# Gate broadcasts of a fused audio tower: source row in SBUF in place of a DRAM scratch

## What is computed

```
h = conv(x)                                   # 8 x 735 x 64
h = h + attention(layernorm(h))
z = layernorm(h)
logits = z @ gate_w + gate_b                  # 16 experts, the best 2 taken
topk_w = softmax(top 2 logits)
hidden = relu(z @ w1[e] + b1[e])              # 64 -> 128, for each expert
moe    = sum over the 2 chosen of topk_w * (hidden @ w2[e] + b2[e])
h = h + layernorm(z + moe) * gamma + beta
```

## Time and profile before

| | |
|---|---|
| median of 3 runs | 476.7 us (476.16 to 478.5) |
| profiled execution | 475.88 us, its span 474.0 us |
| PE busy | 418.6 us, 88% |
| DVE, ACT, POOL busy | 308.5, 164.5, 140.7 us |
| DMA | 55.80 MB, 34.2% of the 16 engines' span |
| broadcasts from DRAM | 128 DMAs of 368 KB, median 8.0 us to landing |
| copies to DRAM | 8 DMAs of 46 KB, median 1.7 us to landing |

### The profile page before, as it was taken

One profiled execution on the slowest core, in us unless ns is written; L12 is line 12 of the kernel. 1 busy time (PEld: TensorE's weight loads), 2 busy tenths in 40 slices (PEclk: granted clock), 3 DMA queues, 4 the chain that ended last, 5 costly groups with the idle time before them and its releaser, 6 DMA issues.

```text
span 474.0 us, 7344 instructions
## 1 busy us (share of the span) xinstructions
PE 418.6 (88%) x2317; PEld 251.1 (53%) x2317; DVE 308.5 (65%) x681; ACT 164.5 (35%) x518; POOL 140.7 (30%) x153
## 2 busy tenths in 40 slices
PE   2839968999999998999999998999899889976991
PEld 1326544655656555665565555655565547543540
DVE  6029456785778567775777577856776677563661
ACT  2134541433344333532452334433362224132021
POOL 3010120104307142524424430724061533064201
PEclk9966968999999999999999999999999899998996
DMA  4801001930077005900193009600670039003900
GB/s 104 152 0 34 1 2 44 381 122 1 5 291 254 17 2 176 367 19 3 59 402 100 0 6 342 208 5 0 229 285 18 1 124 396 9 2 145 385 0 16
DMA packets 42707, 55.80 MB, mean 118 GB/s; under 512 B 23976, under 2 KB 26040, under 8 KB 42680
## 3 DMA queue, kind: packets, MB, share of 16 engines
q1 hardware_dynamic: 42680, 55.46, 34.2%
HBM read 53.57 MB, written 1.88 MB: 117 GB/s over the span
## 4 chain that ended last, share of the span: by engine, by line
PE 64%; DVE 16%; DMA 7%; ACT 5%; issue 5%; POOL 1%; DVEq 0%; POOLq 0%; SPq 0%; ACTq 0%
PE up L939 17%; PE wide L939 14%; PE mix L939 14%; PE small L939 10%; DMA gates_all<-gates_far 5%; DVE row_max L750 3%; DVE hidden L836 3%; DVE prob_sum L761 2%; PE wide L976 2%; DMA gates_far<-gates_t 2%; PE wide L1043 2%; PE small L969 1%; DVE keys L687 1%; ACT cen_sq L511 1%; DVE xn L700 1%
## 5 line engine op out<-in xcount | busy, mean ns | idle before, releaser
L836 DVE SCALAR_TENSOR_TENSOR hidden<-up,b_neg,gates_all 128x368 f32<-128x368 f32 x208 | 115.0, 594 | 45.6 <-PE up L939 34.2
L939 PE MATMUL up<-x,w_hi 128*128 128x368 f32 x256 | 97.7, 381 | 8.0 <-DVE hidden L836 7.0
L939 PE MATMUL mix<-hidden,w2s 128*64 128x368 f32 x512 | 104.2, 498 | 0.0
L939 PE MATMUL up<-x,w_lo 128*128 128x368 f32 x256 | 85.2, 333 | 0.0
L420 POOL TENSOR_SCALAR var_eps<-var 128x6 f32<-128x6 f32 x24 | 5.8, 241 | 250.1 <-ACT cen_sq L511 250.1
L939 PEld LDWEIGHTS up<-x,w_hi 128*128 128x128 f32 x256 | 48.8, 191 | 44.5 <-DVE hidden L836 21.4
L310 POOL TENSOR_TENSOR hidden<-relu,gates_all 128x368 f32<-128x368 f32 x42 | 44.5, 1089 | 40.4 <-ACT relu L552 26.1
L750 DVE TENSOR_REDUCE row_max<-wide 128x1 f32<-128x736 f32 (+1 forms) x48 | 42.9, 918 | 13.4 <-PE wide L939 12.9
L939 PEld LDWEIGHTS up<-x,w_lo 128*128 128x128 f32 x256 | 49.2, 192 | 0.0
L560 ACT ACTIVATE probs<-wide 128x736 f32<-128x736 f32 (+2 forms) x48 | 35.2, 785 | 27.7 <-PE wide L939 27.0
L939 PEld LDWEIGHTS mix<-hidden,w2s 128*64 128x64 f32 x512 | 27.6, 136 | 31.5 <-issue 29.7
(11 more groups left out here) (147 smaller groups left out, 492.1 us busy)
## 6 DMA issues: line engine op xcount, KB each, us to landing
gates_all<-gates_far SPq DMA_DIRECT2D x128, 368.0 KB, 8.0
xx<-x SPq DMA_DIRECT2D x16, 160.0 KB
w_raw<-L_ffn_w SPq DMA_DIRECT2D x2, 512.0 KB, 5.4
out<-outs SPq DMA_DIRECT2D x16, 64.0 KB
w2s<-L_ffn_w SPq DMA_DIRECT2D x1, 512.0 KB, 7.4
gates_far<-gates_t SPq DMA_DIRECT2D x8, 46.0 KB, 1.7
gates_all<-L_tok_w_real SPq DMA_DIRECT2D x1, 256.0 KB, 3.5
gates_all<-L_tok_w_imag SPq DMA_DIRECT2D x1, 256.0 KB, 4.2
```

Of the source, the lines that this page charges most:

```text
L836: dve.scalar_tensor_tensor(hidden[:, e % HIDDEN, s, :], up[s][:, 0:HALF], b1_neg[:, e:e + 1], gates_all[:, e, s * HALF:(s + 1) * HALF], AL ...
L939: return pe.matmul(dst, lhsT, rhs, start=start, stop=stop, skip_group_check=True)
```

## The change

The 16 broadcasts read their row from `gates_t` in SBUF. The source names one partition, repeats it 128 times with a step of zero, and then runs along the 736 numbers. The tensor `gates_far`, the copy to it and SP's wait for that copy are gone. Since the broadcasts now read `gates_t` itself, ACT waits for all 16 of sequence i-1 before it overwrites it for sequence i.

```diff
-        gates_far = nc.dram_tensor("gates_far", (2, E, TOKP), F32, kind="Internal").ap()
...
             def broadcast(i, par, again):
                 sp.wait_ge(s_gtc, i + 1)
-                sp.dma_start(gates_far[par], gates_t[:]).then_inc(s_far, 16)
-                sp.wait_ge(s_far, 16 * (i + 1))
                 sp.sem_inc(s_turn, 1)
                 for e in range(E):
                     if again and e in POOLED:
                         sp.wait_ge(s_phid, CREDIT + hidden_before(i - 1, e, 1, True))
                     elif again:
                         sp.wait_ge(s_hid, hidden_before(i - 1, e, 1, False))
-                    sp.dma_start(gates_all[:, e, :], gates_far[par, e].partition_broadcast(P)).then_inc(s_gall[e], 16)
+                    sp.dma_start(gates_all[:, e, :], gates_t[e:e + 1, :].unsqueeze(1).broadcast_to([1, P, TOKP])).then_inc(s_gall[e], 16)
...
                 if again:
                     act.wait_ge(s_bmm, i)
-                    act.wait_ge(s_far, 16 * i)
+                    for e in range(E):
+                        act.wait_ge(s_gall[e], 16 * i)
                 copy(split(gates_t[:]), wide[0][0:E, :, 0:HALF]).then_inc(s_gtc, 1)
```

More of the change, by code:

```diff
@@ L263, in build @@
         s_gtc = sem("gates_copied")
-        s_far = sem("gates_in_dram")
         s_turn = sem("broadcasts_begun")
```

## The result

The changed kernel takes 1,882.5 us (median of 4 runs, 1,881.7 to 1,884.1) against 477.6 us of the kernel before in the same comparison: 3.94 times as long, 95% interval 3.93 to 3.96. The profiled execution took 1,882.4 us, its span is 1,880.5 us.

A forecast was written before the change was run, and what follows sets the result against it. PE-bound before, the kernel becomes DMA-bound at one row's pace: 78.4 us start, eight sets of 238.7 (1,909.6), 145.6 between them, 13.0 tail, 1.9 around the span, 2,148.5 us; range 1,600 to 2,500.

The forecast's parts named there:

- The burst becomes the bound: DMA broadcasts, until then a burst hidden beside PE, would load the engines almost throughout; DVE waits for `gates_all`.
- The price of a broadcast: 128 packets from one SBUF partition at 117 ns each: 14.9 us a broadcast, 238.7 us a set of 16.
- The reading of the copy: The DRAM copy's 258 ns a packet came from reading source partitions close together, not from writing to DRAM.
- The argument about the store: The store also writes DRAM, in smaller runs, yet moves 14.7 GB/s a busy engine against the copy's 11.3.
- The input queued behind the set: Input of sequence i+2 lands after the broadcasts, PE stands in iterations 1 to 5: 28.4 us each, 142 us.
- ACT's new wait: Before overwriting `gates_t` ACT waits for the previous set's last landing; in iterations 6 and 7 this costs 1.8 us each.
- What the removed copy gives back: Without the copy to DRAM some 5 us would go, if nothing else changed: 471 us.
- Full speed from one partition (1): SBUF gives the row to all 16 engines at full speed: 471 us; 10% for faster, 3% for the same.
- 33 us a broadcast (4): Reads of one partition go at the copy's pace, 33.0 us a broadcast: 4,463 us in all; 5%.
- A single DMA engine (3): The one-partition source puts a broadcast on one engine: again 14.9 us, but a DMA share of 0.06; 8%.
- The input slipping in (5): The input's load lands before the set's end and is not late: 133 us less, 2,015 us; 10%.
- Drifting engines (2): Engines drift apart and read several source rows at once: with half the overlap 159 us a set, 1,512 us; 9%.

The follow-up runs named there:

- copy_by4: Kernel before, its DRAM copy reading 16 partitions four apart of a constant tile, gating left out: 476.0 us against 474.7.
- src16_step4: Changed kernel, each broadcast reading 16 partitions four apart (0 to 60) of a constant tile, 8 times each, gating left out: 505.7 us.
- input_first: Changed kernel with the input load of sequence i+3 issued on SP ahead of the broadcasts of sequence i: 1,775.7 us against 1,882.5.

## Why the prediction came out as it did

The forecast was 2,148.5 us, the range 1,600 to 2,500, the measured time 1,882.5. The mechanism was right in its main parts; one term was too large, and one assumption, that rows never overlap, was wrong without costing much.

- **The burst becomes the bound: right.** DMA share 0.93 inside a set, DVE waiting for `gates_all`, PE for DVE.
- **The price of a broadcast: the step that was mis-sized.** I took the pace of one engine's packet, 117 ns, 14.9 us a broadcast, 238.7 us a set. Measured are 102 ns, 13.0 and 208.1 us. Eight sets: 8 x 30.6 = 245 of the 266 us. So 16 engines on one row draw it somewhat faster than one engine moves a packet; why is open. That it came so close was in part luck. The plateau shows a partition being written at an engine's pace, not one being read, and no row of before shows a read by 16 engines; 14.9 was a choice between 0.93 and 33.0, and nothing there pinned it to 15%. The figure of the Trainium skill (SBUF — State Buffer, Door 1: The DMA port swizzle), which I had kept out of the sum, gave 13.65 us and was the closer one (5% too long, mine 15%).
- **The reading of the copy: right**, and now shown by `copy_by4` and the runs with 16 and 32 sources. The argument about the store pointed the right way. Had I taken the rival's view that the copy's slowness was DRAM's, I would have forecast 471 us.
- **The input queued behind the set: right.** 24.1 us a period and not 28.4 (the terms I listed make 28.3): the input 2.4 us after the last broadcast (284.8 to 287.2, I had 3.5), 20.9 us to the end of ACT's copy (19.0 + 5), and some 1 us to the first packet. The clock cost 1.9 us each and not 5: over this stretch 0.90 was granted. Five times 4.3 is the other 21 of the 266 us.
- **ACT's new wait: right.** It decides iterations 6 and 7: 209.8 - 208.1 = 1.7 us each, 1.8 in the sum. The tail was 14.0 (13.0), the start 77.7 (78.4).
- **What the removed copy gives back: right.** 5 us forecast; 6 us measured with 32 sources, where the sooner landing may have a part.
- **What I would have seen.** Packets some 16 times longer than 117 ns were forecast; the mean was 13 times, the median 14.
- **Rivals.** Full speed from one partition (1) and 33 us a broadcast (4) are out by the set's length. The point that I gave with rival 1, 3.2 us a broadcast, below which a set fits into an iteration, does not decide: at 1.9 us (`src16_step4`) it fits and 27 us are lost. A single DMA engine (3) is out by the share of 0.93. The input slipping in (5) is out by PE's five waits. Drifting engines (2) are the interesting one: in the changed kernel's order four experts in a row lie on one port, and the rate rose only for moments at the change from one four to the next; I gave as the reason that nothing would overlap anyway. The two runs on order show that it was the order, and not a rule of the queue, that kept them together. With the same rows in the other order, or with the rows further apart, the same forecast would have been some 70% too long (2,148.5 us against 1,270.9 and 1,224.5).

The terms as measured: 77.7 + 8 x 208.1 + 5 x 24.1 + 2 x 1.7 + 14.0 = 1,880.4 us, against a span of 1,880.5. That it closes proves little: 24.1 and 1.7 are the measured periods less 208.1, so only the start, one set and the tail are measured apart from the span.

No run here beats the kernel before with its full result. The 6 us are there for a source spread over all partitions, which `gates_t` with its 16 rows is not; 16 sources on eight ports (505.7 and 508.0 us) already lose.

## What to carry to other kernels

Before a DRAM scratch is removed in front of a broadcast, ask how many partitions the new source covers: here one partition fed 128 at 29 GB/s, the DRAM row at 404. The trace of before can answer it if a small DMA with the same source is looked at alone; its packets were twice as long as those of the same size elsewhere. And when a transfer grows long, look at what its queue holds behind it: the input load, free before, cost 21 us in each of five iterations (the 107 us of `input_first`).

## What was not expected of the hardware

- Reordering DMAs on one queue, so that rows that follow one another lie on different source ports, brought 29 to 52 GB/s and took a third off the kernel, with no byte less moved.
- One row read by 16 engines came at 29 GB/s, four neighbouring rows at 24.5 GB/s a port.
- With SBUF sources three to four broadcasts were in flight (44.5 us to landing at 13.0 us each), with the DRAM source, at 8.0 us to landing and 0.93 us each, about nine.
